# Beginning the transfers of the shifted values from ScalarE's queue instead of SP's, in a kernel of a state-space layer and two local-attention layers

## The reference, cut to what matters

```python
qkv = h @ wqkv                      # q, k, v: 8 heads of 64
q, k = l2norm(q) * qs, l2norm(k) * ksc
q, k = rotary_xpos(q, k)
bk, bv = look_around(bk), look_around(bv)      # the window before, and the own one
attn = softmax(where(mask, -max, bq @ bk.T))
out = attn @ bv
x = x + out @ wo
```

## Time and profile before

| | |
|---|---|
| median of 3 executions | 2461.28 us (2460.6 to 2464.99) |
| the profiled execution's own time | 2461.61 us |
| its span, first to last instruction | 2459.8 us |
| busy share of the span | TensorE 77%, VectorE 77%, ScalarE 72%, GpSimd 70% |
| mean granted TensorE clock | 0.943 |
| bytes moved by DMA | 261.09 MB, 16 engines busy 39.6% with the one queue that all DMAs of the kernel use |

### The profile page before, as it was taken

How to read it: one execution, slowest core, us unless ns; L and a number is a source line. 1 busy time by engine, 2 the same in 40 slices (tenths; PEclk the granted TensorE clock), 3 DMA queues, 4 the chain that set the end, 5 groups by cost and what they waited for, 6 DMA issues and landing times.

```text
span 2459.8 us, 44075 instructions
## 1 busy us (share of the span) xinstructions
PE 1893.9 (77%) x15808; PEld 1114.3 (45%) x15936; DVE 1892.7 (77%) x3477; ACT 1778.1 (72%) x3955; POOL 1711.4 (70%) x1540
## 2 busy tenths in 40 slices
PE   2156778797878879797878879697888879787865
PEld 0013345353635445363635445363645545363634
DVE  3557797978879797988878797988879797887442
ACT  2245778696978878696878878696877869685644
POOL 1969595977959596886959596885959597792010
PEclk9977999899999989999999999999999989999988
DMA  4444443535344343534544353534543353531000
GB/s 162 126 120 115 112 105 104 132 83 146 103 130 117 100 121 92 134 86 131 129 129 103 103 124 96 138 87 130 130 115 99 110 127 90 137 99 33 17 20 9
DMA packets 126346, 261.09 MB, mean 106 GB/s; under 512 B 26928, under 2 KB 59696, under 8 KB 125872
## 3 DMA queue, kind: packets, MB, share of 16 engines
q1 hardware_dynamic: 126128, 258.27, 39.6%
HBM read 185.42 MB, written 42.99 MB: 93 GB/s over the span
## 4 chain that ended last, share of the span: by engine, by line
PE 38%; DVE 23%; ACT 13%; issue 9%; POOL 8%; DMA 4%; SPq 0%; DVEq 0%; POOLq 0%; ACTq 0%
DVE hs L618 6%; DVE m L892 4%; PE f_bank L342 4%; PE b_bank L342 4%; DVE kr L906 3%; POOL gy L663 3%; DMA spread<-steps 3%; POOL dbu L646 3%; ACT da L594 3%; PE b_bank L703 3%; PE f_bank L746 3%; PE y_sum L571 2%; DVE b_bank L896 2%; PE b_bank L773 2%; DVE ss L879 2%
## 5 line engine op out<-in xcount | busy, mean ns | idle before, releaser
L618 DVE TENSOR_TENSOR_SCAN hs<-da,dbu 128x512 f32<-128x512 f32 x512 | 622.2, 1215 | 127.1 <-POOL dbu L646 82.0
L663 POOL TENSOR_TENSOR gy<-hs,bc 128x512 f32<-128x512 f32 x512 | 652.1, 1274 | 41.5 <-DVE hs L618 31.2
L646 POOL TENSOR_TENSOR dbu<-spread,bc 128x512 f32<-128x512 f32 x512 | 651.5, 1274 | 9.1 <-DMA spread<-steps 9.0
L594 ACT ACTIVATE da<-spread,rest 128x512 f32<-128x512 f32 x512 | 359.4, 702 | 159.0 <-DVE hs L618 135.1
L703 PE MATMUL b_bank<-rest,h_t 128*128 128x512 f32 x384 | 227.9, 694 | 96.6 <-DVE kr L906 92.5
L960 POOL TENSOR_TENSOR kr<-kr,rn 128x512 f32<-128x512 f32 x256 | 264.8, 1043 | 42.3 <-ACT rn L817 37.0
L703 PE MATMUL f_bank<-rest,h_t 128*128 128x512 f32 x384 | 217.6, 665 | 72.1 <-DVE kr L906 64.2
L571 PE MATMUL y_sum<-gy,rest 128*32 128x512 f32 x1024 | 147.0, 649 | 92.4 <-POOL gy L663 92.3
L342 PE MATMUL f_bank<-first,kr 128*128 128x128 f32 x768 | 128.4, 298 | 78.9 <-DVE kr L906 49.8
L342 PE MATMUL b_bank<-first,kr 128*128 128x128 f32 x768 | 123.7, 296 | 57.8 <-DVE kr L906 41.8
L1106 POOL TENSOR_TENSOR xs<-xs,v 128x512 f32<-128x512 f32 x16 | 18.9, 1183 | 213.3 <-ACT xs L337 213.3
(11 more groups left out here) (168 smaller groups left out, 4748.2 us busy)
## 6 DMA issues: line engine op xcount, KB each, us to landing
spread<-steps SPq DMA_DIRECT2D x256, 512.0 KB, 5.1
vs<-v SPq DMA_DIRECT2D x96, 260.0 KB, 5.9
bc<-bc_rows SPq DMA_DIRECT2D x32, 512.0 KB, 6.2
steps<-k_t SPq DMA_DIRECT2D x32, 512.0 KB, 2.7
gate<-gates SPq DMA_DIRECT2D x32, 512.0 KB, 5.7
gates<-kr SPq DMA_DIRECT2D x16, 512.0 KB, 3.4
gates<-late SPq DMA_DIRECT2D x16, 512.0 KB, 4.3
vs<-v SPq DMA_DIRECT2D x32, 130.0 KB, 4.5
```

What stands on the lines that cost most here:

```text
L594: e.activation(da[:, :], spread[:, slot(b, s // 2), 0, :], ACT.Exp, scale=a_neg[:, s:s + 1]).then_inc(decayed.sem, 1)
L618: e.tensor_tensor_scan(hs[:, s % 2, :], da[:, :], dbu[:, s % 2, :], 0.0, ALU.mult, ALU.add).then_inc(scanned.sem, 1)
L646: e.tensor_tensor(dbu[:, s % 2, :], spread[:, slot(b, s // 2), 1, :], bc[:, s % 2, :], ALU.mult).then_inc(fed.sem, 1)
L663: e.tensor_tensor(gy[:, s % 8, :], hs[:, s % 2, :], bc[:, 2 + s % 2, :], ALU.mult).then_inc(read_out.sem, 1)
```

## The change

The two transfers of each pair are begun on ScalarE's own queue, directly behind the copies of v1 and of v3. ScalarE waits first for its own `v_copied` signal of that tile, since a transfer reads what the copy has written. The function `sp_windows` and the stream A of SP are gone, and SP's word loses the two A1 steps and the first two B1 steps. The order of everything else on SP, and all other engines' words, stay.

```diff
     "sp": (
-        "M1 F2 M5 A1 M1 B1 M1 E1 B1 M3 A1 M6 C1 M5 S3 B1"),
+        "M1 F2 M7 E1 M9 C1 M5 S3 B1"),
 }
...
-        def sp_windows(E, e, b, w):
-            for i in range(2):
-                E.wait_ge(*w.v_copied(b, 2 * i + 1))
-                e.dma_start(w.vs[0:WIN, 2 * i:2 * i + 2, :, :], w.v[0:WIN, 2 * i:2 * i + 2, :, :]).then_inc(w.v_paired.sem, 16)
-                n = min(2, NT - 1 - 2 * i)
-                e.dma_start(w.vs[WIN:, 2 * i + 1:2 * i + 1 + n, :, :], w.v[WIN:, 2 * i:2 * i + n, :, :]).then_inc(
-                    w.v_paired.sem, 16)
-                yield
-
...
                 e.activation(w.v[:, t, :, 0:DH], heads(bank_of(take)[:, :]), ACT.Copy).then_inc(w.v_copied.sem, 1)
+                if t % 2:
+                    E.wait_ge(*w.v_copied(b, t))
+                    e.dma_start(w.vs[0:WIN, t - 1:t + 1, :, :], w.v[0:WIN, t - 1:t + 1, :, :]).then_inc(w.v_paired.sem, 16)
+                    n = min(t + 2, NT)
+                    e.dma_start(w.vs[WIN:, t:n, :, :], w.v[WIN:, t - 1:n - 1, :, :]).then_inc(w.v_paired.sem, 16)
...
-        def sp_front(E, e, b):
-            yield from sp_windows(E, e, b, wf)
-
         def sp_back(E, e, b):
-            yield from sp_windows(E, e, b, wb)
             E.wait_ge(*wb.valued(b, HEADS - 1))
...
-            block.sync(program("sp", dict(C=sp_end, B=sp_back, A=sp_front, M=sp_state, F=sp_steps, E=sp_enter, S=sp_spill)))
+            block.sync(program("sp", dict(C=sp_end, B=sp_back, M=sp_state, F=sp_steps, E=sp_enter, S=sp_spill)))
```

## The result

The changed kernel takes 2538.53 us in the median (2530.54 to 2543.32, four executions) against 2461.48 us of the kernel before (2460.6 to 2464.99). The ratio is 1.0309, 95% interval 1.0282 to 1.0336: 77 us slower. The forecast was 2522 us with a range of 2476 to 2548.

A forecast was written before the change was run, and what follows sets the result against it. No engine bounds throughout; the lead passes between engines in the handwritten order. 14 full rounds of 3.9 us (54.6), plus 3.9, 1.7 and 0.5 us for rounds 14, 15 and -1, give +60.7 us: 2522 us, range 2476 to 2548.

The forecast's parts named there:

- the three places named: In a full round, behind the two v1 tiles, v3 of stream B and v3 of stream A: 1.95, 1.05 and 1.2 us.
- Rivals 3 and 4: 3: issue costs ScalarE nothing, +2 to +7 us, chance 0.11; 4: SP's freed queue makes it faster, 2455 us, chance 0.03.
- rival 1: Local gaps take most; only the v1 delay passes, GpSimd's own work covers v3: 31 us, 2493 us, chance 0.22.
- The price of a pair: On ScalarE, next instruction starts 1.34 us behind the copy's end: SP's 1.24 us for two issues plus two 0.05 us hand-overs.
- Rival 2: The queue pushes back at v1, issues last longer: one a round adds 13 us, 2535 us; two, 2548 us; chance 0.14.
- The sum of a round: Full round, four pairs at three places less SP's gain: 1.95 + 1.05 + 1.2 - 0.3 = 3.9 us.
- the first place: Behind the two v1 tiles: `da` 2.27 us late, VectorE's scan takes it up, 1.95 us reach the round's path.
- The second place: Behind v3 of stream B: squares 1.46 us late, VectorE's L892 and then GpSimd's clip slip, 1.05 us.
- The third place: Behind v3 of stream A: exponentials slip about 1.4 us, passed over TensorE and VectorE's maximum to the next exponentials, 1.2 us.
- What SP gains: SP's queue is freed of four pairs a round, so the load of `spread` goes sooner: -0.3 us a round.
- Rounds 14 and 15: Last rounds: 14, both layers without scan, taken as full, 3.9 us; 15, stream B alone, 1.7 us.

The follow-up runs named there:

- v3 alone: Kernel before with only the pairs of v3 begun by ScalarE, those of v1 by SP as before: 2502.29 us against 2461.1, ratio 1.0169.
- small transfers: Changed kernel with each transfer cut to 16 KB, same issues and places on ScalarE: 2534.98 us against 2463.99 of the kernel before, ratio 1.0283.
- kernels with later places: Changed kernel with pairs issued later: ahead of ScalarE's waits for Q0 and K2, 2465.13 us (ratio 1.0006); behind the squares of k1 and k3, 2484.21 us (1.0099).
- The wait alone: Kernel before with ScalarE also waiting for its own copies of v1 and v3, transfers left on SP: 2461.72 us against 2461.1, ratio 0.9998.

## Why the prediction was right, and where its sum was off

**Direction and mechanism: right.** ScalarE pays for the issues, the slip starts at the three places named, the scan behind `da` is what takes it up first, and the chain shows ScalarE's queue. Rivals 3 and 4 are refuted for this place; rival 1 by v3 alone, which costs 41 us. The size was too small: +60.7 us forecast, +77 measured.

**The price of a pair: right, by luck.** Forecast 1.34 us behind the copy's end. Measured: an undisturbed pair takes 1.19 us (0.03 + 0.47 + 0.03 + 0.61 + 0.05), as the first issue is shorter than on SP, and the long second issues bring the mean of the 64 pairs to 1.36 us. Two errors cancel. Rival 2 foresaw the long issues. Their own bytes, which it named first, are not the cause, since small transfers have them too; the load beside them, which it also named, stays possible.

**The sum of a round: 3.9 us forecast, 5.3 us measured.** The step that was too small is the first place, 1.95 us. Up to the scan it was nearly right: `da` slipped by 2.37 us in the mean (2.27 forecast) and the scan at 1138.46 by 2.10. VectorE carries this 2.1 us unchanged up to 1146, and TensorE starts its next transposes just as late. But the squares that wait for the projection behind these transposes are 3.03 us late, and with them the next `da` and VectorE's scan at 1146.53, which slips by 2.77 us. The 0.67 us between the two scans arise on TensorE. The term left out is TensorE's clock, which the prediction put at nothing. TensorE in that round, before and after:

```profile
1143.23 0.66 PE L342 MATMUL b_bank<-first,kr 128*128 128x128 f32 x4 [2.41 <-DVE kr L906]
1143.72 1.02 PE L703 MATMUL b_bank<-rest,h_t 128*128 128x512 f32 x2
```

```profile
1177.13 1.11 PE L342 MATMUL b_bank<-first,kr 128*128 128x128 f32 x4 [4.57 <-DVE kr L902]
1178.04 1.91 PE L694 MATMUL b_bank<-rest,h_t 128*128 128x512 f32 x2
```

The idle time before the four transposes grew from 2.41 to 4.57 us because VectorE was late, and they and the projection behind them took 1.11 and 1.91 us instead of 0.66 and 1.02. The windows around them give the clock, before and then after:

```profile
1143.00:1146.00 3.00, 1.52 (x6) 0.69 (x6) 3.00 (x5) 2.45 (x6) 3.00 (x3) 1.00 1.04 233
```

```profile
1176.90:1179.90 3.00, 2.77 (x6) 1.25 (x6) 3.00 (x5) 1.46 (x4) 3.00 (x3) 0.50 0.76 209
```

1.00 is the level of 2.4 GHz and 0.50 that of 1.2 GHz: the same work at half the clock. The kernel before also meets a clock of 0.50 in each of its 14 rounds, but in 12 of them only behind these four transposes. At the copy of v3 of stream B the slip is 2.55 us, so 0.2 us of this are gone again.

**The second place: right.** 1.05 us forecast; VectorE's L892 slips by 1.0 us more, and the copy of v3 of stream A by 1.1.

**The third place: 1.2 us forecast, 1.6 measured, and the difference is the clock again.** The exponentials behind v3 of stream A slip by 1.17 us, as forecast. Up to the next exponentials another 0.45 us comes in the mean, and it is not spread evenly: nine rounds gain nothing there, the other five 1.2 to 1.3 us each, and these five are the ones in which the clock falls to 0.50 in that stretch. Two rounds of the changed kernel that follow each other, with the same transposes and the exponentials that wait for their maximum, and the window around them:

```profile
1213.80 1.06 PE L342 MATMUL b_bank<-first,late 128*128 128x128 f32 x4
1218.71 2.17 ACT L853 ACTIVATE late<-b_bank,mx 128x128 f32<-128x128 f32 x8 [1.29 <-DVE mx L918]
1213.50:1216.50 3.00, 2.67 (x24) 1.91 (x23) 1.76 (x4) 2.26 (x6) 2.08 (x3) 0.50 0.13 26
```

```profile
1358.25 0.66 PE L342 MATMUL b_bank<-first,late 128*128 128x128 f32 x4
1362.02 2.17 ACT L853 ACTIVATE late<-b_bank,mx 128x128 f32<-128x128 f32 x8 [0.56 <-DVE mx L918]
1358.00:1361.00 3.00, 2.70 (x56) 2.02 (x55) 2.49 (x5) 2.71 (x8) 1.81 (x3) 1.00 0.13 28
```

Why the clock falls there in five rounds and not in the other nine is not shown. In the kernel before it stays at 1.00 there in all 14. The lengths of the 14 rounds grew by between 3.3 and 7.9 us; the five rounds grew by 7.0 us in the mean, the nine by 4.4.

**What SP gains: -0.3 us a round, not seen.** The waits ended by a landing of `spread` did fall, from 5.1 to 0.4 us on ScalarE. But the three places make 5.29 us and the whole round 5.32, so nothing is left for a gain. Leaving out the transfers altogether, traffic and issues, is worth 7.9 us. One reading beside it was off without harm: the pair of v3 of stream B is issued at 1167.69, lands 3.8 us later and is first read at 1177.2, so 6 us and not 10 before its reader.

**Rounds 14 and 15:** 5.6 us forecast, 6.6 measured, and the agreement is luck: round 14 grew by 2.8 us (3.9 forecast), round 15 by 3.9 (1.7 forecast), of which 2.7 us appear between 2423 and 2431 us of the kernel before, far behind its values.

**The step that the prediction had wrong without harm.** It took the issue on ScalarE as an all-or-nothing choice: paid in full or hidden. The kernels with later places show that it is neither. An issue runs beside instructions already handed over. The own wait right behind the copy keeps it from doing so: the issue starts 0.03 us behind the end of the copy, when nothing is left to run beside. The wait alone is free, the same issues at the later places are nearly free, and the two together right behind the copy cost 77 us. The issues right behind the copy without the wait were not run. That the wait holds them there is read from the timelines of the three places. The Trainium skill (Advanced Engine Details and Errata, section Sequencer Loop) says that engine instructions can be read and queued while a control instruction executes. For a DMA issue on ScalarE the traces show no sign of it: in the changed kernel no ScalarE instruction starts during any of the 128 issues, and those that run beside an issue in the other kernels were queued ahead of it. The Trainium skill (Perfetto Trace Analysis, section Per-engine timelines) says that the sequencer is free for the next instruction only when the descriptors of a DMA have been made, and here the trace agrees: the next instruction starts 0.04 to 0.05 us behind the end of the second issue at the earliest.

## What to carry to other kernels

In these runs a DMA issue on an engine that computes cost that engine what was left of it when the instructions already handed over had ended. Placed behind a wait for the engine's own last result, that was all of it, here 1.2 to 1.4 us a pair. Placed where the data had long been written, with one or two instructions still running and idle time behind, it was close to nothing. Read from the profile what is queued ahead of the issue, what stands behind it and who takes it at once. Then ask what the delay does to TensorE's clock: here it stands behind some 0.9 of the 1.4 us a round that the sum missed.

## What the runs showed of the hardware that was not expected

- A DMA issue on ScalarE's queue began while ScalarE was working on an instruction two places ahead of it (1137.87 against squares that started at 1138.49). Nothing that stood behind an issue started during it.
- The first issue of a pair takes 0.468 us on ScalarE in the median (260 KB or 16 KB) and the second 0.615 us (260 or 130 KB, or 16 KB): the bytes make no difference.
- Some second issues last up to 1.71 us in the changed kernel and 1.52 us with 16 KB. Where ScalarE begins only one transfer at a time, none of the 64 lasts over 0.52 us. What holds the long ones was not settled: in the changed kernel 11 of the 18 over 0.7 us overlap no issue of SP, but all 18 overlap a transfer of SP that has not landed.
- The same four transposes of TensorE took 1.06 us in one round and 0.66 us in the next, at a granted clock of 0.50 and 1.00, and the exponentials behind them waited 0.73 us longer.
